# One masked-maximum instruction over three score banks in a gated cross-attention kernel

## The reference, cut to what matters

```python
q = layernorm(x) @ Wq * scale                  # 16 heads
k, v = split(context @ Wkv)
sim = q @ k.T                                  # per batch, head: 56 x 1500
sim = where(mask, sim, -big)
out = softmax(sim) @ v
x = x + tanh(attn_gate) * (out @ Wo)
x = x + tanh(ff_gate) * gelu(layernorm(x) @ W1) @ W2
```

## Time and profile before

| | |
|---|---|
| median of 3 runs | 2667.14 us (2666.37 to 2675.62) |
| profiled execution: its time, its span | 2673.55 us, 2671.8 us |
| PE busy, share of the span | 94% |
| DVE busy | 59% |
| ACT busy | 47% |
| POOL busy | 22% |
| chain that ended last, by engine | PE 86%, DVE 8%, ACT 2%, DMA 2% |
| TensorE's mean granted clock | 0.95 of full speed |

### The profile page before, as it was taken

How to read it: one execution, slowest core, us unless ns; L and a number is a source line. 1 busy time by engine, 2 the same in 40 slices (tenths; PEclk the granted TensorE clock), 3 DMA queues, 4 the chain that set the end, 5 groups by cost and what they waited for, 6 DMA issues and landing times.

```text
span 2671.8 us, 43128 instructions
## 1 busy us (share of the span) xinstructions
PE 2521.3 (94%) x16890; PEld 2048.4 (77%) x16890; DVE 1572.3 (59%) x4305; ACT 1258.2 (47%) x2148; POOL 590.3 (22%) x729
## 2 busy tenths in 40 slices
PE   7779999999999988988999999899999999999998
PEld 4647999999999667965666666545599999999975
DVE  3146777777776233446766766521577777777741
ACT  2125555555555211116777777520455555555521
POOL 0013444444440004200000000000244444444200
PEclk8789999999999997569999999899999999999999
DMA  8511111111100200001000010101111111111010
GB/s 273 153 49 53 53 39 41 53 38 41 53 27 1 80 18 1 1 3 45 24 24 24 24 34 4 34 31 58 38 41 53 39 41 53 39 41 53 1 48 14
DMA packets 36103, 116.34 MB, mean 44 GB/s; under 512 B 4598, under 2 KB 18526, under 8 KB 35534
## 3 DMA queue, kind: packets, MB, share of 16 engines
q1 hardware_dynamic: 33438, 101.30, 12.2%
q10 hardware_dynamic: 2464, 12.29, 1.8%
HBM read 112.66 MB, written 0.92 MB: 43 GB/s over the span
## 4 chain that ended last, share of the span: by engine, by line
PE 86%; DVE 8%; ACT 2%; DMA 2%; issue 1%; POOL 0%; SPq 0%; ACTq 0%; DVEq 0%; POOLq 0%
PE bank L864 19%; PE bank L851 17%; PE bank L876 11%; DVE n_scores L1635 4%; PE bank L1516 4%; PE bank L1503 3%; PE bank L1528 3%; PE bank L1744 3%; PE bank L1088 2%; PE bank L1073 2%; PE bank L1272 2%; PE bank L683 2%; PE bank L1081 2%; PE bank L1754 2%; PE bank L1253 2%; PE bank L504 2%
## 5 line engine op out<-in xcount | busy, mean ns | idle before, releaser
L924 ACT CAST p_T_high<-bank 125x512 fp32r<-125x512 f32 x672 | 350.6, 595 | 546.8 <-PE bank L876 546.8
L1004 DVE TENSOR_TENSOR p_T_low<-bank,p_T_high 125x512 fp32r<-125x512 f32 x576 | 362.2, 684 | 183.0 <-ACT p_T_high L924 179.5
L864 PE MATMUL bank<-p_T_high,keys_nat_high 125*128 125x256 f32 x1536 | 419.3, 283 | 1.7 <-ACT inverse L931 1.7
L962 DVE CUSTOM_DVE_ANT_0 scores<-bank,mask 128x500 f32<-128x500 f32 x672 | 418.2, 672 | 1.5 <-PE bank L851 1.5
L864 PE MATMUL bank<-p_T_high,keys_nat_low 125*128 125x256 f32 x1536 | 419.1, 283 | 0.0
L934 ACT ACTIVATE scores<-scores,row_max 128x1500 f32<-128x1500 f32 x224 | 353.6, 1578 | 6.5 <-DVE row_max L967 6.5
L876 PE MATMUL bank<-ident,scores 128*125 128x128 f32 x2688 | 330.7, 272 | 1.3 <-ACT scores L934 1.3
L864 PE MATMUL bank<-p_T_low,keys_nat_high 125*128 125x256 f32 x1152 | 325.4, 282 | 0.0
L876 PEld LDWEIGHTS bank<-ident,scores 128*125 128x125 f32 x2688 | 314.2, 188 | 2.7 <-ACT scores L934 2.5
L1635 DVE CUSTOM_DVE_ANT_0 n_scores<-bank,n_zeros 112x500 f32<-112x500 f32 x384 | 237.5, 675 | 127.3 <-PE bank L1503 127.3
L864 PEld LDWEIGHTS bank<-p_T_high,keys_nat_high 125*128 125x128 f32 x1536 | 291.4, 190 | 10.1 <-ACT inverse L931 2.2
(11 more groups left out here) (209 smaller groups left out, 3649.2 us busy)
## 6 DMA issues: line engine op xcount, KB each, us to landing
ctx_T<-in_ctxT SPq DMA_DIRECT2D x40, 750.0 KB, 4.2
ctx_nat<-in_ctx SPq DMA_DIRECT2D x32, 672.0 KB
q_and_o<-in_ctxT SPq DMA_DIRECT2D x16, 750.0 KB, 10.4
q_and_o<-in_ctx ACTq DMA_DIRECT2D x16, 672.0 KB
mask_bytes<-in_mask SPq DMA_DIRECT2D x32, 187.5 KB, 3.0
n_ctx_T<-in_ctxT SPq DMA_DIRECT2D x8, 750.0 KB, 4.4
weights<-in_L_W SPq DMA_DIRECT2D x4, 1024.0 KB, 9.7
ctx_nat<-in_ctx SPq DMA_DIRECT2D x32, 78.0 KB
```

What stands on the lines that cost most here:

```text
L864: m = e.matmul(psum[6 + g % 2][:, 0:256], KNs[i][b % 2][0:KP, cols], PTs[j][g % 2][0:KP, k, :], start=(k == 0 and n == 0), stop=(k == KT - ...
L924: e.copy(PTs[0][g % 2][0:KP, 4 * c:4 * c + 4, lo:lo + 128], psum[3 + c][0:KP, :].rearrange("p (k r) -> p k r", k=4)).then_inc(s_eh, 1)
L962: e.tensor_tensor_reduce(out=SB[u % 2][:, c * CHK:(c + 1) * CHK], in0=psum[c][:, 0:CHK], in1=mb[:, c * CHK:(c + 1) * CHK], scale=1.0, scal ...
L1004: e.tensor_tensor(low, psum[3 + c][0:KP, :].rearrange("p (k r) -> p k r", k=4), high.bitcast(F32), ALU.subtract).then_inc(s_el, 1)
```

## The change

A unit's three banks are declared as one PSUM tensor of 3 x 512 columns, and `scores3` is a view of three rows of 500 columns in it. One instruction takes this view, the mask and `SB` as 3 x 500 and leaves one maximum; it counts the semaphore of the maxima up by three at its end. The reduction over three maxima becomes a multiplication of one number by -1. It waits only for the scores of the third chunk, which PE makes last. Nothing changes on PE, ACT, POOL or SP, and the two other masked maxima of the kernel (layers 0 and 2) stay as they are.

```diff
-        psum = [ctx.enter_context(nc.psum_tensor(f"bank{i}", [128, 512], F32)) for i in range(8)]
+        banks012 = ctx.enter_context(nc.psum_tensor("banks012", [128, 3 * 512], F32))
+        psum = [banks012[:, 512 * i:512 * i + 512] for i in range(3)] + [
+            ctx.enter_context(nc.psum_tensor(f"bank{i}", [128, 512], F32)) for i in range(3, 8)]
+        scores3 = banks012[:, :].rearrange("p (c k) -> p c k", c=3)[:, :, 0:CHK]
...
-                for c in range(CH):
-                    on.wait_ge(*x.scores(u, c))
-                    e.tensor_tensor_reduce(
-                        out=SB[u % 2][:, c * CHK:(c + 1) * CHK], in0=psum[c][:, 0:CHK],
-                        in1=mb[:, c * CHK:(c + 1) * CHK], scale=1.0, scalar=-BIG,
-                        op0=ALU.add, op1=ALU.max, accum_out=mx[:, u % 4, c:c + 1]).then_inc(s_mx, 1)
+                on.wait_ge(*x.scores(u, 2))
+                e.tensor_tensor_reduce(
+                    out=SB[u % 2].rearrange("p (c k) -> p c k", c=CH), in0=scores3,
+                    in1=mb.rearrange("p (c k) -> p c k", c=CH), scale=1.0, scalar=-BIG,
+                    op0=ALU.add, op1=ALU.max, accum_out=mx[:, u % 4, 0:1]).then_inc(s_mx, 3)
                 on.wait_ge(*x.maxima(u, 2))
-                e.tensor_reduce(mx[:, u % 4, 3:4], mx[:, u % 4, 0:3], AX.X, ALU.max, negate=True).then_inc(s_nx, 1)
+                e.tensor_scalar(mx[:, u % 4, 3:4], mx[:, u % 4, 0:1], -1.0, None, ALU.mult).then_inc(s_nx, 1)
```

## The result

The changed kernel takes 2674.16 us in the median of 20 runs (2666.37 to 2680.22), the kernel before 2666.82 us (20 runs, 2657.78 to 2676.33). The ratio is 1.0027, with a 95% interval of 1.0016 to 1.0037: about 7 us or 0.27% slower, which is less than the 0.5% that I called measurable, but clear with so many runs. It lies in the predicted range, 4 us above the predicted time. The loss is 2.6 times the 2.8 us of my sum, and the time stands nearer to the 2672 to 2674 us that I had given the clock rival than to the forecast.

A forecast was written before the change was run, and what follows sets the result against it. PE was taken to bound the attention loops, with VectorE's saving off the path. Steady state 0 plus 2 x 1.4 = +2.8 us at the loop starts, carried to the median of 2667.14, gave 2669.9 us; range 2665 to 2679.

The forecast's parts named there:

- the clock rival: First steps of each loop: longer standing still keeps PE's clock low, 2 to 4 us on top, 2672 to 2674 us; chance 0.18.
- the forecast: Both loops: steady state hidden, 1 to 3 us lost at the starts, 2669.9 us; chance 0.70.
- What bounds the kernel: Inside both attention loops PE sets the pace, standing still 1.85 of 1248 us, while VectorE always has time over.
- The waits before: Score matmuls waited for a maximum three times in 224 units, 2.6 us in all, so about 3 us to win.
- The work itself: VectorE's maxima: one instruction of 1.68 us replaces three, saving 0.50 us a unit, 112 us of busy time over 224 units.
- Cover in the middle: Mid-loop steps: value sums and transposes hide the banks' later return with 1.44 us left, so steady state costs 0.
- The first steps of each loop: No value sums cover the late maximum before unit 3, so PE waits: 1.4 us a loop.
- unit 3 starts at 1931.83: Second loop: unit 3's scores start there instead of at 1930.47, 1.36 us late, after waiting for unit 2's maximum.
- The slow instruction: Every step: PE waits if the large instruction passes 3.12 us, chance 0.03; dear but covered, 2676 us, chance 0.04.
- the gain of VectorE's time: Rival: VectorE's 112 us were on the path, in whole or part; in whole 2555 us; chance 0.02.
- the split: Rival: the view is split into three instructions again, leaving only the late start, 2667 to 2670 us; chance 0.03.
- L1321 as the upper bound: A dearer VectorE row, 1.70 ns a column, would make the large instruction 2.72 us, 1.04 more than in the sum.

The follow-up runs named there:

- e1: Changed kernel with the old three maxima kept in units 0 to 2 of each loop; 1.0008 of the kernel before.
- e2: Kernel before with the one instruction only in units 0 to 2 of each loop, six in all; 1.0047 of the kernel before.
- e5: Changed kernel with a needless copy of 880 score columns ahead of the one instruction in every unit; 1.0052 of the kernel before.
- e7: Changed kernel with the reciprocal of units 0 to 2 ahead of the next unit's maximum; one run, 2669.70 us.
- e6: Changed kernel with a needless copy of 1500 score columns ahead of the one instruction in every unit; 1.0429 of the kernel before.
- e8: Changed kernel with three maxima in units 0 to 2, first low parts behind unit 0's maxima, 22 identity transposes before its scores; 1.0007 of the kernel before.
- e4: Changed kernel with identity transposes into idle bank 7 where PE waits for the maxima of units 0 to 2; 1.0030 of the kernel before.

## Why the prediction was right, and where it was off

The range held, and in part by luck: it was 14 us wide, to take in the scatter, around an expected 2.8 us. The mechanism, cover in the middle and waits in the first steps, is shown by e1, e2 and e5 to e7. The size of the forecast, 1 to 3 us, was not right; 7 us came, 4.5 of them from the starts and the rest with the clock.

- **What bounds the kernel**: right. PE keeps its pace in the middle of both loops, and e1 shows that 218 of the 224 new instructions cost nothing.
- **The waits before**: misread. The "three times, 2.6 us" of the earlier trace rows are one matmul's 0.55 us and two weight loads ahead of matmuls in the same pauses, so PE had about 0.5 us to win there and not 3.
- **The work itself**: the length was right (1.72 us against 1.68; it had to pass 3.12 to matter), the saving on VectorE was not: 14 us of busy time instead of 112. I multiplied durations of instructions that overlap each other. It cost nothing here, as the saving was not on the path.
- **Cover in the middle**: right, mis-sized by 0.2 us (1.25 for 1.44). I took 0.04 us from PE's last matmul to VectorE's start, from a row of the old instruction; the new one starts 0.17 us behind it (514.68 to 514.85). The clock is not the reason, as behind a matmul at 1.2 GHz it is 0.18 (220.82 + 0.62 = 221.44, start at 221.62); what the reason is stays open. e5 and e6 put the edge between 1.0 and 1.6 us of added delay.
- **The first steps of each loop**: right mechanism, mis-sized term. It was 1.36 us a loop in the sum and 2.24 us on the chip at equal clock. The step that failed is "unit 3 starts at 1931.83": I had the score matmul wait for the maximum but forgot the spread, which waits for a reciprocal queued behind that maximum. e7 takes it out and gives 0.33 us back. The later starts of VectorE in three steps, 0.14, 0.11 and 0.14 us more than the 0.04 of my sum, make up most of the remaining 0.55.
- **The clock as a rival**: I gave it 0.18 and 2 to 4 us, and it came true: with it I had 2672 to 2674 us, and 2674.16 were measured. My sum put the clock at nothing. In all three profiles of the changed kernel at least one start is longer than 14.77 us (16.59; 16.36 and 15.47; 16.57), where the kernel before has 12.5 us in five of six. What I did not see is that stages downstream change too, about 2 us in the queries and, in two of three profiles, 1.5 us in the projections. "In the middle of the loops PE never pauses, so nothing there can lose the clock" was right and beside the point: the clock was also lost in stages that I had not looked at.
- **The slow instruction, the gain of VectorE's time, the split**: none happened. There are 224 instructions of 1500 columns and no wait in the middle.
- **L1321 as the upper bound**: too far off. By it a column cost 1.70 ns; measured, 1000 more columns took 1.721 - 0.672 = 1.05 us, 1.05 ns each. The Trainium skill's rule that jumps between runs cost nothing ("Vector Engine (DVE) Microarchitecture Reference", section 5.2) stands there for operands in SBUF; the two jumps of this case are in PSUM, and its 1.721 us agrees with the rule there too.

## What to carry to other kernels

Fewer and longer instructions on an engine that is not the bound win nothing, and one that waits for the last of three inputs and returns all three buffers at once takes the overlap away; look for the places where nothing covers that, which are the first steps of a pipeline. Follow each short instruction queued behind the long one as well (here a reciprocal) to whoever waits for it. And where a matmul engine's clock moves between two levels, a change that costs 2 us in one stage can come with as much again in others, and chance in a stage ahead of it can be larger than both (here 11 us). So a stage by stage table of several profiles says more than one span.

## What was not expected of the hardware

- Behind the first loop, stages with identical instructions had one of a few sharp lengths and nothing between: the queries of layer 3 took 42.3 to 42.4 us or 44.0 to 44.6 us, and in the profiles of the tables the last stage took 101.9 to 102.1 or 103.7 to 103.8; which one went with the kernel upstream. In the queries the difference is the granted clock, 1.00 or 0.50, in the first 3 us after a pause.
- Layer 0, ahead of all that, has no such lengths: 108.6 to 120.9 us in twelve profiles, 110.1 to 120.9 in three of one and the same kernel.
- The scatter of a kernel's runs, 15.4 us from end to end in the 43 later runs of the kernel before, goes mostly with the mean granted clock: 2.0 us for 0.001.
- With 22 transposes that nobody reads ahead of the scores, PE kept its clock at 1.00 through both starts (e8), where it fell in every other profile. In e4, with such transposes in a pause of 2 us, unit 1 to 2 took 4.33 us in both loops, where one loop without them had 6.15; in the whole kernel nothing was gained.
